# First attention's turns by source and its gate prepared early, the embedding reordered, pairs norm by thirds, switch choice in two parts

## The reference

```python
h = concatenate([cls_tok, patch_embedding(x, W)])       # x is (2, 64, 128, 64)
# layer 0 attention, on the layernorm of h
xr, xw, xk, xv, xa, xg = [x + delta * x_mix[i] for i in range(6)]
r = xr @ W_r; k = xk @ W_k; v = xv @ W_v
w = DECAY_SCALE * sigmoid(tanh(xw @ A_w) @ B_w + b_w)
a = sigmoid(xa @ A_a @ B_a + b_a)
g = sigmoid(xg @ A_g) @ B_g
kk = normalized(k * k_k); k = k * (1.0 + (a - 1.0) * k_a)
o = scan(step, S0, (r, exp(w), k, v, kk, a))
o = (o - mu) * rsqrt(var + EPS) * gn_w + gn_b
o = o + sum(r * k * r_k) * v
h = h + o * g @ W_o
...
# layer 2 attention: 32 heads of 2 numbers; q and k normalized pair by pair
q = _rmsnorm(heads(q), qn_w); k = _rmsnorm(heads(k), kn_w)
# layer 2 feed-forward: one of 32 experts for each token
idx = argmax(xf @ router_w.T + router_b)
out = relu(relu(xf @ W1[idx] + b1[idx]) @ W2[idx] + b2[idx])
```

## Time and profile before

| | us |
|---|---|
| median of three runs | 1396.93 |
| lowest and highest | 1394.74, 1402.99 |
| profiled execution | 1403.48 |
| its span, first to last instruction | 1401.8 |
| PE, DVE, ACT, POOL busy | 1082.6, 907.7, 764.8, 165.7 |

### The profile page before, as it was taken

How to read it: one execution, slowest core, us unless ns; L and a number is a source line. 1 busy time by engine, 2 the same in 40 slices (tenths; PEclk the granted TensorE clock), 3 DMA queues, 4 the chain that set the end, 5 groups by cost and what they waited for, 6 DMA issues and landing times. The chain is left out here.

```text
span 1401.8 us, 27715 instructions
## 1 busy us (share of the span) xinstructions
PE 1082.6 (77%) x11369; PEld 613.5 (44%) x11369; DVE 907.7 (65%) x1939; ACT 764.8 (55%) x1072; POOL 165.7 (12%) x176
## 2 busy tenths in 40 slices
PE   5857956544879879946999999969799999996250
PEld 3646944433444444441333333354455556555120
DVE  0677467867980367765675555454799999974524
ACT  0451323213117643358999999932488898982020
POOL 0006303220002200000000000010024000000514
PEclk9978887766559989956999999978899999998565
DMA  8000000040000000000000000010000000002021
GB/s 156 20 1 1 4 4 18 4 69 6 3 1 1 1 0 1 1 2 3 1 2 1 2 1 2 1 40 3 1 2 2 2 2 2 2 2 68 15 45 27
DMA packets 42818, 18.24 MB, mean 13 GB/s; under 512 B 38069, under 2 KB 41641, under 8 KB 42437
## 3 DMA queue, kind: packets, MB, share of 16 engines
q1 hardware_dynamic: 40965, 15.39, 5.4%
q0 software_dynamic: 1728, 1.08, 0.4%
HBM read 12.95 MB, written 3.48 MB: 12 GB/s over the span
## 5 line engine op out<-in xcount | busy, mean ns | idle before, releaser
L2553 ACT ACTIVATE pt_PT<-ps 128x1024 f32<-128x1024 f32 x288 | 266.1, 1104 | 5.7 <-PE ps L2623 5.4
L3545 DVE TENSOR_SCALAR da_AD<-da_QH,da_XG,da_XH 128x1024 f32<-128x1024 f32 x296 | 231.2, 848 | 16.0 <-PE ps L3702 15.4
L3593 ACT ACTIVATE da_AD<-ps,da_NX 128x1024 f32<-128x1024 f32 x214 | 221.1, 1184 | 29.4 <-PE ps L3702 29.1
L3702 PE MATMUL ps<-da_AD,dw_win 128*32 128x256 f32 x4080 | 230.6, 382 | 4.6 <-DVE da_AD L3545 2.3
L3702 PEld LDWEIGHTS ps<-da_AD,dw_win 128*32 128x32 f32 x4080 | 130.2, 110 | 102.3 <-DVE da_AD L3545 15.1
L2589 PE MATMUL ps<-pt_PT,pa_V 128*32 128x512 f32 (+3 forms) x1536 | 155.1, 497 | 8.3 <-DVE pt_Yc L2530 3.2
L2537 DVE TENSOR_TENSOR pt_PT<-pt_PT,pt_keep 128x512 f32<-128x512 f32 x128 | 84.2, 689 | 61.3 <-ACT pt_PT L2553 60.1
L2623 PE MATMUL ps<-pt_QT,pt_KT 12*128 12x512 bf16 (+3 forms) x768 | 80.1, 334 | 3.2 <-DVE pt_KT L2495 0.5
L2589 PEld LDWEIGHTS ps<-pt_PT,pa_V 128*32 128x32 f32 x1536 | 38.8, 109 | 64.7 <-issue 63.2
L2162 ACT ACTIVATE mt_act<-ps 128x342 f32<-128x342 f32 (+1 forms) x66 | 30.1, 456 | 53.7 <-PE ps L2217 53.7
L2217 PE MATMUL ps<-mt_XF,ew_w 64*128 64x342 f32 (+1 forms) x132 | 54.2, 494 | 0.8 <-ACT mt_WT L2148 0.8
(11 more groups left out here) (790 smaller groups left out, 2065.3 us busy)
## 6 DMA issues: line engine op xcount, KB each, us to landing
em_xs<-in_x_dram SPq DMA_DIRECT2D x2, 1152.0 KB, 14.7
em_xs<-in_x_dram SPq DMA_DIRECT2D x2, 1024.0 KB, 19.1
cp_xbuf<-ci_zero SPq DMA_DIRECT2D x1, 672.0 KB
cp_XS<-cp_xbuf SPq DMA_DIRECT2D x8, 84.0 KB, 2.1
cp_ybuf<-cp_YS SPq DMA_DIRECT2D x8, 84.0 KB, 2.1
ew_win<-in_L_ffn_w_dram SPq DMA_DIRECT2D x2, 320.0 KB
em_WS<-in_L_tok_W_dram SPq DMA_DIRECT2D x8, 72.0 KB
la_blk<-la_scratch SPq DMA_DIRECT2D x8, 64.1 KB
```

The source lines that it names most:

```text
L2553: nc.scalar.activation(PT[:, n % RING, 2 * i:2 * i + 2, :], ps[:, b0:b0 + 2, :], ACT.Exp, scale=SCALE).then_inc(exp_ok, 1)
L3545: nc.vector.tensor_scalar(AD[:, j % RING], QH[:, b], XG[:, b, s:s + 1], XH[:, b, s:s + 1], ALU.max, ALU.subtract).then_inc(ad_dve, 1)
L3593: nc.scalar.activation(AD[:, j % RING], QA, ACT.Abs, bias=NX[:, b, s:s + 1]).then_inc(ad_act, 1)
L3702: ins = nc.tensor.matmul(o, D.win[:, int(by[j] == "D"), hp, 15 - m:47 - m], AD[:, j % RING, hp], start=False, stop=False, skip_group_check ...
```

## The change

In the embedding each batch's result is copied half by VectorE and half by ScalarE (embedded). Batch 0's turns stand ahead of batch 1's products. The weights' loads wait until batch 1 of x has landed, and mixed moves behind batch 0's norm. In the projections ScalarE takes the sigmoid first and copies the upper half of batch 1's S, and VectorE's copies of S alternate with those of the hidden groups. rwkv_scaled turns all KK, then all Rt, then all BK, in 15 units of up to four tiles through seven banks; ScalarE copies twelve units and VectorE three, and VectorE writes -KK. The bonus moves to the end of the first chunk block. The second chunk block begins with (v * bonus + gn_b) * gate, written over TM's w, and gate * gn_w, written over the gate; the output keeps two passes of five. In the pairs the norm goes by thirds with the squares on ScalarE, the zeros are filled by POOL, and the halves and epsilons of the mean go into Sqrt's scale and bias. The switch's weights are loaded, masked and centred during the pairs' attention, its choice is made in parts of 6 and 12 tiles, four of the six turns of xo move into the loop, the products go through three banks, and ScalarE takes all of the first eight products.

```diff
+        def embedded(eng, copy, b, half, done):
+            eng.wait_ge(emb_ps, b + 1)
+            XV = XT[:, b * PADSEQ + 1:b * PADSEQ + SEQ].rearrange("p (v n) -> p v n", n=16)
+            copy(XV[:, :, 8 * half:8 * half + 8],
+                 ps[:, 4 + 2 * b + half, :].rearrange("p (n v) -> p v n", v=64)).then_inc(done, 1)
+
...
+                sp.wait_ge(x_in[1], 32)
                 R.load(nc, sp, A)
...
+                pad(0)
+                embedded(dve, nc.vector.tensor_copy, 0, 0, emb_sb)
+                pad(1)
+                dve.wait_ge(h_ok, 3)
+                R.variance(nc, link, K.h, 0, var_ready)
+                link(R.normed(nc, dve, link, 0, std_ready))
+                R.mixed(nc, dve, link)
+                embedded(dve, nc.vector.tensor_copy, 1, 0, emb_sb)
...
+                        pe.wait_ge(emb_sb, 1)
+                        pe.wait_ge(emb_act, 1)
+                        for g in range(3):
+                            turn(g)
+                pe.wait_ge(emb_sb, 2)
+                pe.wait_ge(emb_act, 2)
...
-                for g in range(3):
-                    hidden(g)
                 for g in range(3, NG):
+                    hidden(g - 3)
                     dve.wait_ge(tr_ps, g + 1)
-                    nc.vector.tensor_copy(S[0:64, 1, cols(g, 0)], ps[0:64, TURNS[g], 0:GRP])
-                    nc.vector.tensor_copy(S[64:128, 1, cols(g, 1)], ps[64:128, TURNS[g], 0:GRP]).then_inc(s_dve, 1)
+                    nc.vector.tensor_copy(S[0:64, 1, cols(g, 0)], ps[0:64, TURNS[g], 0:GRP]).then_inc(s_dve, 1)
...
-                    act.wait_ge(hid_ps, 2 * g + 1)
-                    nc.scalar.activation(H1[0:64, c], ps[0:64, HIDS[g], 0:GRP], ACT.Tanh).then_inc(sig_sb, 1)
                     act.wait_ge(hid_ps, 2 * g + 2)
                     nc.scalar.activation(H2[:, c], ps[:, HIDS[g] + 1, 0:GRP], ACT.Sigmoid).then_inc(sig_sb, 1)
+                    nc.scalar.activation(H1[0:64, c], ps[0:64, HIDS[g], 0:GRP], ACT.Tanh).then_inc(sig_sb, 1)
+                    if g < 3:
+                        act.wait_ge(tr_ps, g + 4)
...
+        UNITS = [(j, t0, min(4, T - t0)) for j in range(3) for t0 in range(0, T, 4)]
+        RBANK = (7, 0, 1, 2, 3, 4, 5)
+        DUNITS = (10, 12, 14)
+
+        def turned(eng, copy, u, done):
+            j, t0, n = UNITS[u]
+            eng.wait_ge(tr_ps, u + 1)
+            copy(QT[:, t0:t0 + n, j, :], ps[:, RBANK[u % len(RBANK)], 0:n * P].rearrange("p (a b) -> p a b", a=n)
+                 ).then_inc(done, 1)
...
-                link(tt(tmp[:], TM[:, :, K_], bc(rows[:, 4], T), ALU.mult))
-                link(tt(tmp2[:], tmp[:], TM[:, :, R_], ALU.mult))
-                link(nc.vector.tensor_reduce(bonus[:], tmp2[:], AX.X, ALU.add))
+                for u in DUNITS:
+                    turned(dve, nc.vector.tensor_copy, u, tr_dve)
+                nc.vector.tensor_scalar(Y[:, :, 64:128], KK, -1.0, None, ALU.mult)
...
-                for t in range(T):
-                    act.wait_ge(tr_ps, t + 1)
-                    nc.scalar.copy(flat(QT[:, t]), ps[:, t % 4, 0:GRP]).then_inc(tr_sb, 1)
-                nc.scalar.activation(Y[:, :, 64:128], KK, ACT.Identity, scale=-1.0)
+                for u in range(len(UNITS)):
+                    if u not in DUNITS:
+                        turned(act, nc.scalar.copy, u, tr_act)
...
-                pe.wait_ge(kk_twice, 1)
-                pe.wait_ge(r_twice, 1)
-                pe.wait_ge(scaled, 4)
-                for t in range(T):
-                    if t >= 4:
-                        pe.wait_ge(tr_sb, t - 3)
-                    for j, src in enumerate((KK2, Rt2, BK)):
-                        ins = nc.tensor.transpose(ps[:, t % 4, j * P:(j + 1) * P], flat(src[:, t]), ident[0:P, 0:P])
+                pe.wait_ge(e_ok, 3)
+                for u, (j, t0, n) in enumerate(UNITS):
+                    if t0 == 0:
+                        pe.wait_ge((kk_twice, r_twice, scaled)[j], (1, 1, 4)[j])
+                    if u >= len(RBANK):
+                        pe.wait_ge(tr_act, u - len(RBANK) + 1 - sum(d <= u - len(RBANK) for d in DUNITS))
+                    for t in range(t0, t0 + n):
+                        ins = nc.tensor.transpose(ps[:, RBANK[u % len(RBANK)], (t - t0) * P:(t - t0 + 1) * P],
+                                                  flat((KK2, Rt2, BK)[j][:, t]), ident[0:P, 0:P])
...
+                    link = Chain(dve, vch)
+                    link(tt(TM[:, :, K_], TM[:, :, K_], bc(pre["rows"][:, 4], T), ALU.mult))
+                    link(tt(TM[:, :, W_], TM[:, :, K_], TM[:, :, R_], ALU.mult))
+                    link(nc.vector.tensor_reduce(bonus[:], TM[:, :, W_], AX.X, ALU.add))
...
+                link(tt(own, TM[:, :, V_], bcl(bonus[:], 64), ALU.mult))
+                link(tt(own, own, bc(pre["gn"][:, 1], T), ALU.add))
+                link(tt(own, own, gate, ALU.mult))
+                link(tt(gate, gate, bc(pre["gn"][:, 0], T), ALU.mult))
...
-                link(tt(on[:], on[:], bc(gn[:, 0], T), ALU.mult))
-                link(tt(on[:], on[:], bc(gn[:, 1], T), ALU.add))
-                link(tt(tmp[:], TM[:, :, V_], bcl(bonus[:], 64), ALU.mult))
-                link(tt(on[:], on[:], tmp[:], ALU.add))
-                tt(on[:], on[:], TM[:, :, G_], ALU.mult).then_inc(o_ok, 1)
+                link(tt(on[:], on[:], TM[:, :, G_], ALU.mult))
+                tt(on[:], on[:], TM[:, :, W_], ALU.add).then_inc(o_ok, 1)
...
+    def load(self, sp, A):
+        E = self.E
+        sp.dma_start(self.rin[:], A["L2_ffn_router_w"]).then_inc(self.in_, 16)
...
+    def mask(self, nc, pool):
+        link = Chain(pool, self.nil)
+        E, XR = self.E, self.XR
+        for a in (self.W1[XR:128], self.b2[0:64], self.b2[XR:128]):
+            link(nc.gpsimd.memset(a, 0.0))
+        pool.wait_ge(self.in_, 16 * self.LOADS)
+        w, e = self.W1[64:64 + E].rearrange("p (e f) -> p e f", e=E), self.eye[64:64 + E]
+        link(nc.gpsimd.tensor_tensor(w, w, bcl(e, self.FF), ALU.mult))
+        link(nc.gpsimd.tensor_scalar(e, e, -1.0, self.BIG, ALU.add, ALU.mult))
+        nc.gpsimd.tensor_tensor(w, w, bcl(e, self.FF), ALU.add).then_inc(self.masked, 1)
...
+    def centre(self, nc, dve, link):
+        dve.wait_ge(self.in_, 16 * self.LOADS)
+        link(nc.vector.tensor_reduce(self.rmean[:, 0:1], self.rin[:], AX.X, ALU.add))
+        link(nc.vector.tensor_scalar(self.rmean[:, 1:2], self.rmean[:, 0:1], 1.0 / 64, None, ALU.mult))
+        link(nc.vector.tensor_scalar(self.rin[:], self.rin[:], self.rmean[:, 1:2], None, ALU.subtract))
...
+                pool.wait_ge(eps_ok, 3)
                 nc.gpsimd.memset(V1[:], 1.0).then_inc(ones_ok, 1)
+                for k, a in enumerate((Q12, K12)):
+                    pool.wait_ge(ones_ok, k + 1)
+                    nc.gpsimd.memset(a[:].rearrange("p t h e -> p (t h) e").bitcast(F32)[:, :, 6:16], 0.0
+                                     ).then_inc(ones_ok, 1)
...
-                layernorm_dve(nc, dve, link, K.h[:], xn[:], tmp[:], st[:], var_ready, std_ready)
-                nc.vector.tensor_copy(st[:, 0, :], st[:, 3, :]).then_inc(x_ok, 1)
+                third = lambda q: slice(6 * q, 6 * q + 6)
+                nc.vector.memset(each[:], 1.0 / 64).then_inc(eps_ok, 1)
+                nc.vector.memset(eps[:, 0:1], 1e-5).then_inc(eps_ok, 1)
+                nc.vector.memset(eps[:, 1:2], 1e-6).then_inc(eps_ok, 1)
+                dve.wait_ge(eps_ok, 3)
+
+                def centre(q):
+                    s = third(q)
+                    link(nc.vector.tensor_reduce(st[:, 0, s], K.h[:, s], AX.X, ALU.add))
+                    link(tt(st[:, 0, s], st[:, 0, s], each[:, s], ALU.mult))
+                    tt(xn[:, s], K.h[:, s], bcl(st[:, 0, s], 64), ALU.subtract).then_inc(xc_ok, 1)
+
+                def variance(q):
+                    s = third(q)
+                    dve.wait_ge(xsq_ok, q + 1)
+                    nc.vector.tensor_reduce(st[:, 1, s], tmp[:, s], AX.X, ALU.add).then_inc(var_ready, 1)
+
+                def rows_out(q):
+                    s = third(q)
+                    dve.wait_ge(std_ready, q + 1)
+                    link(nc.vector.reciprocal(st[:, 3, s], st[:, 2, s]))
+                    tt(xn[:, s], xn[:, s], bcl(st[:, 3, s], 64), ALU.mult).then_inc(x_ok, 1)
+
+                centre(0)
+                centre(1)
+                variance(0)
+                centre(2)
+                rows_out(0)
+                variance(1)
+                rows_out(1)
+                variance(2)
+                rows_out(2)
...
-                    nc.vector.tensor_scalar(pm[:, g], pm[:, g], 0.5, 1e-6, ALU.mult, ALU.add).then_inc(m_ok, 1)
+                    nc.vector.tensor_reduce(pm[:, g], sq[:, g].rearrange("p t (h e) -> p t h e", e=2),
+                                            AX.X, ALU.add).then_inc(m_ok, 1)
...
-                pads(Q12)
-                root_act(nc, act, st[:], var_ready, std_ready)
...
```

(33 more changed lines are left out.)

273 lines of the change are left out of this document (138 added, 135 removed).

## The result

The changed kernel took 1384.19 us (median of 6 runs, 1379.97 to 1386.59) beside 1397.08 us for the kernel before: ratio 0.990, 95% interval 0.988 to 0.992. Forecast was 1378 within 1370 to 1389. The first profiled execution took 1385.75 us, its span is 1384.0.

A forecast was written before the change was run, and what follows sets the result against it. Six blocks have six limits, mostly chains of waits between TensorE, VectorE and ScalarE. Terms +1.0 - 2.5 - 4.8 - 4.2 - 2.2 + 0.3 - 6.3 = -18.7 us took 1396.93 to 1378.2 us, range 1370 to 1389.

The forecast's parts named there:

- Embedding: First block: later weights' loads delay the last turns, less a copy's gain; +1.0 us, from -0.6 to +3.
- Projections: Projections: shorter wait for S (1.4 us) and full clock behind it (1.6 us); -2.5 us, from -1.4 to -3.0.
- Scaled operands: rwkv_scaled: TensorE's turns start with KK at 87.5, not waiting for BK until 91.63; -4.8 us, from -4.0 to -5.1.
- Gate and bonus: Output loses three VectorE passes of 1.36 us, moved work filling idle gaps elsewhere; -4.2 us.
- The rival of slipping passes: Gate and bonus: a gap closes and the output's 4.2 us come back, giving 1382.4 us; chance 0.07.
- Pairs: Pairs' preparation: norm by thirds, first third ready at 6.4 us instead of 8.6; -2.2 us, from -1.2 to -3.
- The fills: Pairs' preparation: POOL's zero fills hold VectorE's norm, +6.7 us, giving 1384.9 us; chance 0.09.
- Attention: Pairs' attention: added loads, masks and small VectorE operations, collisions mostly covered; +0.3 us, 0 to +1.5.
- Switch: Switch: first product 8.3 us sooner, 2.0 given back in the loop; -6.3 us, from -4.5 to -7.5.
- the slower rival: Switch's loop: TensorE's clock stays at 1.2 GHz, 31 us more, giving 1409.2 us; chance 0.04.
- Little arrives: Fills hold the norm (+6.7 us) and three banks slow the switch's loop (+6.4 us), giving 1391.3 us; chance 0.06.
- A sign of being wrong: Untouched blocks (two middle layers, distance stage) changing by more than the runs' spread would show the prediction wrong.

The follow-up runs named there:

- the two later ones: The changed kernel unchanged, timed twice more against the kernel before: ratios 0.9865 and 0.9876, medians 1381.57 and 1381.45 us.
- the copy first: Changed kernel with two embedding lines exchanged, VectorE copying batch 1 before scaling the weights: 1376.23 us, ratio 0.9839 to the kernel before.
- the masks behind the cast: Changed kernel with copy exchanged, -KK earlier, POOL's masks after the identity's cast: ratio 0.9838 to before; with token loads also earlier, 0.9833.
- filling them: Changed kernel with 25 unread identity products in TensorE's four waits ending the pairs' attention: ratio 0.9892, beside 0.9865 for the changed kernel.

## Why the prediction came out as it did

**The sum** was right within 1.5 us of the averaged traces (-18.7 against -17.2), and so was the sign of every term. The point lies 6 us under the first median because that comparison gave -13, where the two later ones gave -19.4 and -18.8, with the kernel before 3 to 4 us slower beside them and the changed one 3 faster; single executions of the kernel before lay anywhere from 1391.7 to 1407.3 us. Nothing that repeats in the traces asks for the smaller value, and the first interval reaches to -16.6. The closeness of the sum is in part luck: the projections and the attention of the pairs gave 2.0 us less than forecast and the embedding 0.6, the pairs' norm and the switch 1.1 more.

**Embedding** (+1.0, measured +1.6): the later start of the turns came out at 1.0, by two steps that were off in opposite ways. x was to land 1.3 us sooner and the gain in start is 0.4; the table's way from issue to landing was to take 3 us and took 1.86. The mix table came at 39.87 (41.4 forecast, 39.5 to 43 the marker), the wait on VectorE is there, and the turns start 1.0 us later on the mean of six traces (43.5 against 42.5). Not in the sum was the half clock of the turns behind that wait, another 0.6.

**Projections** (-2.5): this is the term that failed, and with it my range for it (-1.4 to -3.0, measured -1.2). The step was "at full clock this is 3.8 us": I counted 1.6 us for a warm stretch that three of four traces of the kernel before have without any change (3.83 us, shows the fourth). The second step that failed is the other 1.4 us, the turn's wait. The wait went, but the turn came only 0.35 us sooner on the mean (8.23 us into the block before, 7.89 in six traces of the changed order), because the hidden products ahead of it ran below full clock: that stretch shows 0.63 to 0.76 in all six, and 1.00 in two of the four traces before. At equal clock 1.3 of the 1.4 is there: with the copy first, three traces at 1.00 have the turn 6.61 us into the block, and two of the kernel before, also at 1.00, have it at 7.95. A further 0.4 us that the prediction put at nothing came behind TM's first product (17.16 us to the running sums and not 17.55); no run says by which edit. Behind the turn, the low clock of the first trace was a state of that execution and not a cost of the code, and belonged in the range and not in the term; ahead of the turn the order of the embedding may have a part in it.

**Scaled operands** (-4.8): measured -4.8. The first turn came 11.25 us behind the running sums against 15.27, and TensorE was the bound, as forecast; a copy took 0.54 us where I bounded it by 0.63. I had VectorE write -KK in 0.7 to 1.36 at the end, and it took 0.75 there, though it had been idle 2.66 us before its copies.

**Gate and bonus** (-4.2): measured -4.17 in the output, in every trace. The rival of slipping passes, which would give the 4.2 us back, is out, but the passes do slip a little where the clock is high. In three of ten traces the four gate passes fill their gap and VectorE's first instruction for the states comes 5.83 us into the block, against 5.61 in the two fastest traces of the kernel before: 0.2 us. In five of ten the three bonus passes end their block, which then goes over to the next one 0.6 us behind ScalarE's last copy and not 0.3. What is left of the cover, counted as 2.4 us, is 2.7 to 3.0 us in four of the ten traces and nothing in those three.

**Pairs** (-2.2): measured -2.8, within the range. The first third was ready 5.8 us into the block, 0.6 sooner than worked out; the three small operations at the start took 0.15 us together where I had taken 0.4, and the two scalings 0.17 each.

**The fills**: the rival is out, no pass beside a fill exceeds 0.56 us. The Trainium skill (SBUF — State Buffer, Who interferes with whom) says that a VectorE instruction with two SBUF inputs contends with a GpSimd instruction that reads SBUF and not with one that only writes it, while a cast can enter a mode that contends with GpSimd. The traces agree on all three: 0.56 beside the fill, 1.17 beside POOL's tensor operation, 0.56 instead of 0.23 for the cast beside a memset.

**Attention** (+0.3): 0.34 of it is that cast at the block's start, which delays the first Exp from 5.48 to 5.82 us behind it (5.48 again in both traces with the masks behind the cast); I had looked for collisions in the masking and not at the head of the chain. The other 0.6 is a later rise of TensorE's clock in the first 15 us, in five of seven traces (280.6 us against 279.6). With the masks behind the cast the block took 279.12 us in one trace and 280.09 in the other, so it comes and goes there too.

**Switch** (-6.3): measured -6.8. The start was right (11.54 us against 11.5), the second part of the choice was hidden as forecast, and the loop gave back 1.2 and not 2.0. The loop ran at 1.00, so the slower rival is out. "Little arrives" is out too: no fill held the norm, and the loop took 1.1 us more than before on the mean and not 6.4.

**A sign of being wrong** was named that came up: a block that nothing touches, the second layer's attention, took 66.89 us in the first trace of the changed kernel and 68.67 to 68.75 in the other thirteen. It did not come again, so it belongs to that execution and not to the change.

**Open**: what sets the clock. In the embedding's last turns and the hidden groups up to the projections' last turn it stayed at 1.00 in all three traces where the turns waited 0.89 us (the exchanged copy), in two of six where they waited 1.4 to 1.7 us, and in none of the five where they waited 3.4 to 3.5 us. In the output product it stood at 0.50, 0.72 or 1.00 behind the same waits, and filling them did not help.

## What to carry to other kernels

Take the length of a block from more than one trace before a term rests on it, and where PEclk is below 1.00 in one of them, price the edit at both clocks. When a wait for a transfer is added to one queue, follow who stands behind the instruction that first needs it: here the late load did no harm by itself, and the order of two VectorE instructions cost 2.6 us of waiting (3.5 against 0.89). Work with no reader in the block (-KK, masks, a gate) goes into the idle time that the timeline shows, ahead of the last copies; what else its engine stops at that hour is to be read too, as with the masks beside the cast.

## What the hardware showed that I had not expected

TensorE's granted clock is the largest source of spread that these traces show: the same turns and products took 5.7 us at 1.00 and 10.8 at 0.50, in two executions of one kernel. POOL's memset more than doubles a VectorE cast of 128 columns (0.23 to 0.56 us) and leaves a subtraction of 384 columns alone (0.56). A product of two 128-column float32 operands leaves two rows in the trace (22 for 11, in 2.72 us), and takes 0.25 us at full clock where I had taken 0.1. And 0.2 KB issued behind 4.3 MB on the same queue took 21 to 23 us.
